# GpSimd clears a small buffer and waits for it between the scatters of an edge sort and the gathers of six edge sums

## The reference, cut to what matters

```python
def _scatter_add(tgt, idx, src, axis=0):
    return tgt.at[idx].add(src)
def _segment_sum(src, seg, n):
    return jax.ops.segment_sum(src, seg, n)
...
# one attention layer over edges (one of four graph layers, two of which have two)
e = jax.nn.leaky_relu(alpha_src[src] + alpha_dst[dst], NEG_SLOPE)
m = jax.ops.segment_max(e, dst, num_segments=n)
e = jnp.exp(e - m[dst])
s = jax.ops.segment_sum(e, dst, num_segments=n)
alpha = e / (s[dst] + 1e-16)
out = jax.ops.segment_sum(alpha[:, :, None] * h[src], dst, num_segments=n)
```

## Time and profile before

| what | before |
|---|---|
| median of 3 runs | 10622.69 us (10619.56 to 10624.97) |
| span of the profiled execution | 10685.8 us |
| TensorE matmul busy | 6666.1 us, 62% |
| VectorE busy | 5067.1 us, 47% |
| ScalarE busy | 2678.2 us, 25% |
| GpSimd busy | 3649.9 us, 34%, 3597 instructions |
| mean granted TensorE clock | 0.773 of full |

### The profile page before, as it was taken

The page is one execution under the profiler, slowest core; times in us unless marked ns, Lnnn a source line. Parts: engine busy times, 40 slices in busy tenths (PEclk is TensorE's granted clock), DMA queues, the critical chain, the costliest instruction groups (busy, mean ns, idle before and its releaser), DMA issues. The chain is left out here.

```text
span 10685.8 us, 95917 instructions
## 1 busy us (share of the span) xinstructions
PE 6666.1 (62%) x27702; PEld 4202.5 (39%) x27702; DVE 5067.1 (47%) x10547; ACT 2678.2 (25%) x6047; POOL 3649.9 (34%) x3597
## 2 busy tenths in 40 slices
PE   5456656689657536649984663665664577626856
PEld 4452333334444433336753332333443233313434
DVE  6453046522477733461126544436545788733231
ACT  0012100022244404302223430331222455312211
POOL 2522346400246436602032763462111355120021
PEclk5558877799779857769996776677787799868968
DMA  3110033210246433304423333331022122210012
GB/s 94 38 34 13 4 89 91 56 46 27 69 136 179 120 98 88 91 6 131 168 83 96 95 90 78 101 91 32 15 67 61 44 68 69 68 58 7 7 60 76
DMA packets 440710, 758.91 MB, mean 71 GB/s; under 512 B 172573, under 2 KB 268795, under 8 KB 437521
## 3 DMA queue, kind: packets, MB, share of 16 engines
q0 software_dynamic: 182080, 437.26, 15.1%
q1 hardware_dynamic: 239987, 295.32, 8.8%
q10 hardware_dynamic: 18136, 20.19, 0.6%
HBM read 669.59 MB, written 82.56 MB: 70 GB/s over the span
## 5 line engine op out<-in xcount | busy, mean ns | idle before, releaser
L2448 POOL DMA_INDIRECT R<-table,edges x1248 | 1243.2, 996 | 861.0 <-issue 306.3
L2500 DVE TENSOR_TENSOR acc<-acc,PS 125x256 f32 (+3 forms) x1664 | 704.9, 424 | 1242.4 <-PE PS L2519 376.5
L2519 PE MATMUL PS<-R,hot 128*125 128x256 f32 (+1 forms) x1664 | 644.8, 476 | 418.0 <-issue 203.4
L2527 PE MATMUL PS<-iota_b,ident_b 128*128 128x500 bf16 x1728 | 764.7, 449 | 5.7 <-PEq L71 5.7
L2268 PE MATMUL PS<-S,hotT 125*128 125x100 bf16 (+1 forms) x6240 | 362.9, 218 | 575.1 <-DVE hotT L2375 460.4
L2460 ACT ACTIVATE R<-R,TW 128x128 f32<-128x128 f32 (+1 forms) x1248 | 493.4, 431 | 685.0 <-DMA R<-table,edges 644.7
L2519 PEld LDWEIGHTS PS<-R,hot 128*125 128x125 f32 x1664 | 361.6, 234 | 683.1 <-issue 520.3
L2517 PE MATMUL PS<-R,hot 128*125 128x258 f32 x1664 | 438.0, 416 | 203.6 <-DVE acc L2498 117.5
L2268 PEld LDWEIGHTS PS<-S,hotT 125*128 125x128 bf16 x6240 | 315.3, 112 | 623.8 <-DVE hotT L2375 429.7
L2448 POOL DMA_INDIRECT xx<-table,edges x416 | 412.8, 992 | 384.4 <-PE PS L2519 312.5
L2448 POOL DMA_INDIRECT room<-table,edges x416 | 425.6, 1023 | 330.2 <-PE PS L2519 191.7
(11 more groups left out here) (719 smaller groups left out, 13558.8 us busy)
## 6 DMA issues: line engine op xcount, KB each, us to landing
rowb<-slo_row SPq DMA_DIRECT2D x260, 250.0 KB
W<-in_L_ffn_W1p SPq DMA_DIRECT2D x32, 1024.0 KB
W<-in_L_ffn_W2p SPq DMA_DIRECT2D x32, 1024.0 KB
near<-dst_row SPq DMA_DIRECT2D x98, 256.0 KB
R<-table,edges POOLq DMA_INDIRECT x1248
W<-in_L_ffn_w SPq DMA_DIRECT2D x16, 1024.0 KB
hib<-hi_mask SPq DMA_DIRECT2D x260, 50.0 KB
g<-gate_rows POOLq DMA_DIRECT2D x8, 1568.0 KB
```

What stands on the lines that cost most here:

```text
L2448: pool.indirect_dma_start(self.R[:, u, 0:self.W], None, self.table[:, :], bass.IndirectOffsetOnAxis(ap=self.G.edges[:, g, 0:1], axis=0)).t ...
L2500: v.tensor_tensor(to, to, self.G.PS[0:P, self.bank + k, 0:self.WH], ALU.add).then_inc(self.put, 1)
L2519: mm = pe.matmul(self.G.PS[0:P, self.bank + k, 0:self.WH], hot, self.R[:, u, :], start=True, stop=True)
L2527: pe.matmul(G.PS[:, 6, 0:4 * P], G.ident_b[:, :], G.iota_b[:, :].unsqueeze(1).to_broadcast([128, 4, P]), start=True, stop=True)
```

## The change

Behind every scatter of the sort and every gather of the edge sums, GpSimd clears a buffer of 128 partitions by 32 float32 and waits until that clearing is done. The buffer is read by nobody. A semaphore is added for the sort, and one for each sum.

```diff
@@ class Scatter
+        self.rest, self.rested = s.sb("rest", [128, 32]), s.sem("rested")
 
     def send(self, pool, f):
         pool.indirect_dma_start(self.G.sorted[:, :], bass.IndirectOffsetOnAxis(ap=self.place[:, f:f + 1], axis=0),
                                 self.rows[:, f, :], None).then_inc(self.scattered, 16)
+        pool.memset(self.rest[:, :], 0.0).then_inc(self.rested, 1)
+        pool.wait_ge(self.rested, f + 1)
@@ def gather
         pool.indirect_dma_start(self.R[:, u, 0:self.W], None, self.table[:, :],
                                 bass.IndirectOffsetOnAxis(ap=self.G.edges[:, g, 0:1], axis=0)).then_inc(self.got[u], 16)
+        pool.memset(self.rest[:, :], 0.0).then_inc(self.rested, 1)
+        pool.wait_ge(self.rested, g + 1)
```

## The result

| what | before | after |
|---|---|---|
| median of 3 runs | 10622.69 us | 10553.64 us (10542.14 to 10566.25) |
| span of the profiled execution | 10685.8 us | 10564.5 us |
| mean granted TensorE clock | 0.773 | 0.803 |

The ratio is 0.9934, with a 95% interval of 0.9916 to 0.9952: 69 us less, where 382 had been forecast. The two profiled executions differ by 121 us, since that of before lies 63 us above its median and that of after 12.

What follows compares the result with a forecast made beforehand. GpSimd's close indirect DMAs were taken to make TensorE's semaphores late. Sums +29, sort -184, mix0 -110 and edge weights -117 gave -382 us, 10240 us from 10622.7; own range 10040 to 10485, 8-in-10 range 10000 to 11000.

Steps and rivals of the forecast that it cites:

- What goes away, if the theory holds, is the close run.: Long, close runs of indirect DMAs make TensorE's semaphores late; spacing them ends this, and TensorE, VectorE and ScalarE keep up.
- p: New distance between gather starts: 0.995 + 0.10 + 0.12 + 0.28 = 1.50, taken as 1.52 us; forecast's range 1.43 to 1.63.
- Sort: VectorE at its pace without scatters, GpSimd ending last, at 567 instead of 751 us: -184 us.
- mix0: Feed-forward matmuls at full pace beside the scatters, ending about 1195 instead of 1306 us: -110 us.
- Edge weights: VectorE regains the steps lost beside the gathers sent ahead, 52 + 43 + 22 us: -117 us.
- Five sums: GpSimd's pace sets the stage: 1968 x 1.52 us plus 5 x 3 us, against 2977.6: +29 us.
- whole relief: The forecast's own case: semaphores no longer late at the new distance, up to 1.65 us; 10240 us, chance 0.58.
- It breaks even at p = 1.505: Five sums: rests between gathers alone gain nothing; above this distance they lose, each 0.1 us being 197 us.
- Half relief: Rival: VectorE at half pace while GpSimd sends, as beside line 2215; -36 us in all, 10587 us; chance 0.12.
- No relief: Rival: lateness follows the number of indirect DMAs, not spacing, so clearings only add cost; +663, 11290 us; chance 0.09.
- A dear pause: Rival: relief as forecast, but a distance of 1.7 to 1.9 us; about 10640 to 11090 us; chance 0.08.
- a wait for the transfer: Rival: the clearing waits until the gather's data have landed, distance 3.4 us; 15400 us; chance 0.08.

Runs made afterwards that it cites:

- second group: Two or three clearings (1.0039, 1.0070) or a pause every sixth (1.0019), at scatters and early gathers; two everywhere (1.0378); against the kernel before, 9800.26 us on that chip.
- double rest: Two clearings of 128 x 96, each with its wait, behind every scatter and gather, against the kernel before: 11355.67 us, ratio 1.0680.
- third chip: Kernel before, unchanged: 10689.22 us; against it the change 0.9967, and behind scatters and early gathers only, three clearings 0.9688, two 0.9808.

## Why the prediction was off

The direction was right and the size was not: -382 us forecast, -69 measured. The step that failed is the relief; the distance was off too, by less. The link between close runs and late news, on which the forecast rests, holds.

**"What goes away, if the theory holds, is the close run."** That the relief would be whole at the new distance was taken, not worked out. The trace of before had only 1.25 us and, at line 2215, 1.49 us with half the pace. What the runs show is a steep curve: the next stage after the sort starts at 751 us with a distance of 1.25, at 726 to 730 with 1.37 (three traces), at 693 with 1.44 and at 584 with 1.50. The change stops short of the steep part.

**The distance.** The sum for p had a gap of 0.10 us in front of the clearing and put 0.12 + 0.28 us behind an already mean gather of 0.995: 1.52. The trace has no gap: 1.02 + 0.14 + 0.27 = 1.43 in the mean, the low end of the range given for p, and 1.37 undisturbed. The idle 0.30 us that follows every gather is not a fixed cost to which the clearing is added; the clearing takes place in it and the wait has its own 0.27. By the forecast's reasoning the shorter rest would have been better still (2233 x 0.09 = 201 us less, 10040 us). It was worse, because of the first step.

**The sum at its own distance.** Three clearings everywhere have a mean of 1.52 us in the sums, just the p of the forecast, and test the rest of its terms. Sort: forecast -184, measured -168 (751.5 to 583.5); there GpSimd ends last, as forecast. mix0: -110, measured -113 (311 to 198, from the first scatter to the next stage); there too the scatters end last, as forecast. Edge weights: -117, measured -34, -13 and -35 us in the three stages, -82. Five sums: +29, measured +77 (3054.8 against 2977.6). That makes -286 of -382, and with 13 us less in the other stages it is the 299 us by which the span is below that of before. The change didn't reach the distance at which these terms apply.

Two terms were mis-sized. The edge weights were priced at the pace that VectorE has with GpSimd idle, 52 steps in 60 us; beside gathers that delay nothing it makes 40 (second group), and whole relief is worth 96 us (double rest) and not 117. In the sums the pace held (1.52 us), but the forecast allowed 15 us for all that comes beyond it, and 61 were measured.

**The sums.** "It breaks even at p = 1.505" supposes that nothing is late below that. In after 1968 x 1.43 would be 2814 us; measured are 2982. The windows, here to the end of the last matmul, can be split into GpSimd's own pace (the gathers and the least idle time behind each), its waits beyond that, and what follows the last gather:

| five sums, us | own pace | waits | after the last gather |
|---|---|---|---|
| before | 2563 | 298 | 118 |
| after | 2822 | 76 | 86 |
| three clearings everywhere | 2996 | 24 | 37 |

What came off the waits went into the rests. On the third chip, where both kernels can be compared, the change's sums are 38 us longer, so the forecast's +29 came near for another reason than its own: GpSimd's pace is 1.43 and not 1.52 us, and the lateness is still there.

**The rivals.** Half relief, 10587 us, was nearest: mix0 -33 (measured -57, on the third chip -39), edge weights -32 (-34; -7), sort 0 (-25; -26), sums +29 (+4; +38). It had been given 0.12, against 0.58 for whole relief, though the row at 1.49 us spoke for it. But it was meant for p = 1.52, and there the sort gains 168 us and not 0; that its number came near at 1.43 is luck. No relief had its mark at fewer than 10 steps beside the early gathers; 13 were made, 10 on the third chip, and the double rest shows the relief whole. A dear pause and a wait for the transfer fell with the first rows of the timeline.

**The rule weighed.** The Trainium skill, "SBUF — State Buffer", section "Who interferes with whom", says that PE and ACT never wait on anyone. It says so of ports, and on three of four chips it does not hold as a rule for the time of this kernel: what waits on TensorE starts late beside close indirect DMAs (ScalarE in mix0 by 9.9 us in the mean), however it comes about. On the chip of the second group the trace agrees with it: 104 to 112 records in the sort beside the scatters, as many as without them.

**Open.** What holds the news back is not shown, nor why one chip, or one time, has nothing of it. Scatters and gathers of quite different row widths both do it, which speaks for the number of rows and not the bytes, but no run varied that alone. The change itself was not run on the chip without lateness; two clearings everywhere cost 3.8% there, so a cost is likely. The profiled run of rests behind the scatters alone had mix0 at 198 us, the two of the change at 250 and 268 with the same scatters; this spread is not explained, and it makes any single trace of mix0 at 1.37 us a poor measure. The distances 1.37, 1.44 and 1.50 us were not all timed on one chip with the same places: only 1.44 and 1.50 were.

## What to carry to other kernels

Before a pause is bought, read in the trace what it costs per operation and how many places stand on the path: put it where the victims are (sort, early gathers) and not where the pausing engine is itself the bound (the sums). Relief by spacing can be steep, so measure it at three or four distances, not one; here 0.13 us more than the change's, at the same places, took the gain from 0.7% to 2.1%, and without the rests in the sums to 3.1%. And time such a cure on more than one chip: on the chip without the illness it was only a cost.

## What the runs showed of the hardware

- The same kernel before took 10623 to 10692 us on three chips and 9800 us on a fourth, that of the second group. In the traces (before, and the kernel with two clearings on that fourth chip, spans 853 us apart) the difference lies where GpSimd sends indirect DMAs: the five sums, gathers 1.25 us apart in both, take 2606 and not 2978 us, the sort ends 190 us earlier, mix0 is 120 us shorter, the edge weights 152 us and the sixth sum 20 us: 853 in all.
- On the other three chips TensorE's news comes late beside indirect DMAs 1.25 us apart: in before ScalarE in mix0 starts 9.9 us late in the mean (up to 26.9), VectorE in the first sum 0.61 us (up to 7.4). With 1.50 us these are 0.04 and 0.14 us, the values of the fourth chip at 1.25 to 1.50 us; with 1.7 to 2.0 us the edge weights run at their full pace beside gathers, also when no clearing but a wait for a landing makes the distance.
- A clearing starts at the end of an indirect DMA's record without a gap; without a wait it costs nothing (distance 1.26 us). A further one of 128 x 32 adds 0.06 us without a wait between them, 0.18 with one (four clearings, each with its wait, take 0.69 us). The next DMA, if it waits, starts 0.27 us behind the clearing, 0.52 in the sums with two waits of the double rest.
